# Content rows of attention made two groups at a time and moved on the chip by DMA

## What is computed

```python
h = layernorm(x) * (1 + ca) + sa
x = x + ga * attention(h)          # 16 heads, 16 content and 64 rope columns each, causal
h = layernorm(x) * (1 + cb) + sb
x = x + gb * ffn(h)                # 8 chosen experts of 96, weighted by a router
```

## Time and profile before

| | us |
|---|---|
| median of 3 runs | 1072.28 (1072.27 to 1074.97) |
| the profiled execution | 1072.48 |
| its span, first to last instruction | 1070.4 |
| PE busy | 1007.9 (94%) |
| DVE busy | 767.8 (72%) |
| ACT busy | 403.3 (38%) |
| POOL busy | 413.9 (39%) |
| mean granted TensorE clock | 0.981 |

### The profile page before, as it was taken

One profiled execution on the slowest core, in us unless ns is written; L12 is line 12 of the kernel. 1 busy time (PEld: TensorE's weight loads), 2 busy tenths in 40 slices (PEclk: granted clock), 3 DMA queues, 4 the chain that ended last, 5 costly groups with the idle time before them and its releaser, 6 DMA issues.

```text
span 1070.4 us, 24879 instructions
## 1 busy us (share of the span) xinstructions
PE 1007.9 (94%) x9783; PEld 735.9 (69%) x9783; DVE 767.8 (72%) x1518; ACT 403.3 (38%) x731; POOL 413.9 (39%) x357
## 2 busy tenths in 40 slices
PE   5979989999899999999899998999999998999888
PEld 4656667766686667766677666876768766776566
DVE  6767688586967868677776769768686777866454
ACT  4334533254314443145341643235431444315320
POOL 1526442264405454055432634145540644316200
PEclk9989999999999998999899999999999999999999
DMA  6220000200002000200002000020001000010000
GB/s 195 60 90 2 2 1 1 70 2 2 1 2 70 2 1 1 70 2 2 1 1 71 1 2 1 1 71 1 2 1 43 29 2 1 1 50 2 2 1 20
DMA packets 22232, 23.59 MB, mean 22 GB/s; under 512 B 6314, under 2 KB 20138, under 8 KB 22130
## 3 DMA queue, kind: packets, MB, share of 16 engines
q1 hardware_dynamic: 22130, 22.02, 6.7%
HBM read 17.80 MB, written 4.21 MB: 21 GB/s over the span
## 4 chain that ended last, share of the span: by engine, by line
PE 72%; DVE 11%; issue 8%; POOL 4%; ACT 3%; DMA 1%; POOLq 0%; DVEq 0%; SPq 0%; ACTq 0%
PE ring L1158 15%; PE ring L1006 11%; PE ring L1007 9%; PE ring L1008 9%; PE ring L1235 8%; PE av L1174 7%; PE ring L1130 5%; DVE mcol L888 2%; ACT pt L694 2%; POOL prod L564 2%; DVE xr L927 2%; PE ring L1142 2%; PE av L1187 1%; PE ring L1224 1%; DVE room L908 1%
## 5 line engine op out<-in xcount | busy, mean ns | idle before, releaser
L694 ACT ACTIVATE pt<-ring 128x384 f32<-128x384 f32 (+1 forms) x384 | 170.8, 532 | 316.9 <-PE ring L1158 281.2
L579 POOL TENSOR_SCALAR_AFFINE_SELECT pt<-pt 128x512 f32<-128x512 f32 x128 | 79.5, 637 | 391.9 <-ACT pt L694 391.9
L864 DVE TENSOR_TENSOR prod<-ring,table 128x1024 f32<-128x1024 f32 x128 | 155.5, 1218 | 92.7 <-PE ring L1008 92.1
L888 DVE TENSOR_REDUCE mcol<-ring 128x1 f32<-128x128 f32 (+3 forms) x512 | 211.4, 481 | 12.8 <-PE ring L1135 9.6
L1158 PE MATMUL ring<-rows 32*128 32x512 f32 (+3 forms) x3072 | 177.3, 331 | 10.0 <-ACT pt L694 5.0
L1158 PEld LDWEIGHTS ring<-rows 32*128 32x128 f32 x3072 | 131.6, 184 | 61.6 <-issue 30.0
L570 POOL TENSOR_TENSOR rows<-prod,rows 128x1024 fp32r<-128x1024 f32 x64 | 152.7, 2395 | 34.6 <-ACT rows L674 34.6
L563 POOL TENSOR_TENSOR prod<-prod 128x512 f32<-128x512 f32 x64 | 82.4, 1287 | 134.9 <-DVE prod L864 133.8
L1130 PE MATMUL ring<-rows 32*128 32x256 f32 (+3 forms) x1024 | 78.4, 356 | 21.6 <-ACT cont L686 6.9
L674 ACT ACTIVATE rows<-prod 128x1024 fp32r<-128x1024 f32 x64 | 67.6, 1063 | 58.3 <-PE ring L1158 36.9
L1130 PEld LDWEIGHTS ring<-rows 32*128 32x128 f32 x1024 | 44.5, 185 | 61.9 <-issue 42.2
(11 more groups left out here) (169 smaller groups left out, 1630.6 us busy)
## 6 DMA issues: line engine op xcount, KB each, us to landing
xn<-x_dram SPq DMA_DIRECT2D x8, 512.0 KB, 3.9
xr<-x_dram SPq DMA_DIRECT2D x8, 512.0 KB, 4.2
out_dram<-xr SPq DMA_DIRECT2D x8, 512.0 KB, 3.2
gate_bc<-gates_scratch SPq DMA_DIRECT2D x8, 256.0 KB, 4.8
pt<-wmod_dram SPq DMA_DIRECT2D x1, 1536.0 KB, 6.4
pt<-gup_t_dram SPq DMA_DIRECT2D x16, 96.0 KB, 2.5
dn<-wu_t_dram SPq DMA_DIRECT2D x1, 640.0 KB, 10.0
xr<-wk_t_dram SPq DMA_DIRECT2D x1, 512.0 KB, 8.2
```

The costliest lines, as they stand in the source:

```text
L694: sc.activation(pt[:, PT_AT[n] + h * w:PT_AT[n] + (h + 1) * w], ps[:, 0:w], ACT.Exp, scale=SCALE).then_inc(exp_ready.sem, 1)
L864: ve.tensor_tensor(prod[:, s % PROD, :, :], ps[:, :].unsqueeze(1).broadcast_to([P, 2, S]), table[:, :, :], ALU.mult).then_inc(rotated.sem, 1)
L888: last = ve.reduce_max(mcol[:, q, h * HR + HD:h * HR + HD + 1], ps[:, at:at + (q + 1) * P], AX_X)
```

## The change

1. The content columns are no longer laid out twice: `CON` is 256, and one `qcon` or `kcon` product (128 columns) holds two groups, the even group on even partitions and the odd group on odd ones. There are two of each for a block (p = 0, 1) instead of four.
2. `kcon_hi`/`kcon_lo` and `qcon_hi`/`qcon_lo` write hi and lo to `k_split` and `q_split`, which are the buffers `h2_hi` and `h2_lo` in the time in which the FFN does not use them. New steps `move_k` and `move_q` on SP, one of each for every group, copy every second partition to `cont`, three DMAs of 64 rows of 2 KB (128 KB) each.
3. `wofold` (POOL) multiplies `wo` by the gate into `wo_gated` (in the buffer `xn`), once for a block; `mixed` only adds.
4. The three orders are new, and blocks 1 to 6 are generated one after the other instead of a hardware loop. `load_late` gathers the late loads of the setup behind the first moves.

The diff, cut to its core:

```diff
-CON = NG * P
+CON = H * HD
+NBLK = CON // P
 SETUP_ORDER
-... kcon.00 kcon_hi.00 kcon_lo.00 ... qcon.00 qcon_hi.00 qcon_lo.00 ... kcon.01 kcon_hi.01 kcon_lo.01 hi.010 maxima.000 ... fuse.4 fuse.5 qcon.01 qcon_hi.01
-qcon_lo.01 shift.00 shifted.00 hi.011 lo.011 spread. split_ffn.0 split_ffn.1
+... kcon.00 kcon_hi.00 kcon_lo.00 move_k.00 ... qcon.00 qcon_hi.00 qcon_lo.00 move_q.00 rope.0101 rotate.0101 combine.010 values.00 values_out.00 values.01 values_out.01 move_k.01 hi.010 maxima.000 ... fuse.4 fuse.5 move_q.01 shift.00 shifted.00 hi.011 lo.011 spread. split_ffn.0 split_ffn.1 load_late.
 BODY_ORDER
-load_next.1 loads.0 maxima.010 rope.0200 reduce.010 score.000 ... combine.021 value.000 value.001 reduce.012 score.002 hi.020 shift.01 qcon.02 lo.020 exp.002 kcon.02 ...
+rope.0200 score.000 rotate.0200 load_next.1 rope.0201 exp.000 score.001 rotate.0201 clear.000 stats1.1 value.000
+exp.001 maxima.010 kcon.01 pow1.1 reduce.010 rope.0210 kcon_hi.01 clear.001 combine.020 score.002 rotate.0210
+kcon_lo.01 value.001 exp.002 maxima.011 hi.020 rope.0211 reduce.011 clear.002 maxima.012 rotate.0211 qcon.01
+reduce.012 combine.021 rope.0300 qcon_hi.01 shift.01 lo.020 value.002 shifted.01 qcon_lo.01 score.010 move_q.02
+attn_out.00 rotate.0300 rope.0301 loads.0 move_k.02 exp.010 score.011 rotate.0301 hi.021 clear.010 exp.011 maxima.020
...
+value.021 reduce.031 maxima.032 rope.1000 wofold.0 reduce.032 score.022 rotate.1000 shift.03 exp.022 rope.1001
...
+qcon_hi.10 value.032 qcon_lo.10 kcon.10 move_q.10 attn_out.03 values.10 rope.1011 values_out.10 hi.100 mix.00
+rotate.1011 kcon_hi.10 lo.100 kcon_lo.10 mix.01 move_k.10 mixed.00 combine.101 move_q.11 rope.1100 mixed.01 move_k.11
+hi.101 stats2.0 rotate.1100 pow2.0 maxima.100 lo.101 norm2.0 rope.1101 reduce.100 turn2.00 turn2.01 values.11
...
+wo_gated = xn[:, 0:NPAIR, :]
+k_split, q_split = h2_hi, h2_lo
+        def split_free(e, moved, b, ahead, p):
+            if p:
+                wait(e, up_used, b, ahead - 1, FT - 1)
+            for par in range(2):
+                wait(e, moved[par], b, ahead if p else ahead - 1, 2 if p else 3 * NBLK - 1)
-                with e.Fori(1, B - 1) as b:
+                for b in range(1, B - 1):
 SP
+                    elif kind in ("move_k", "move_q"):
+                        g = step[2]
+                        par, p = g % 2, g // 2
+                        if part != "setup":
+                            heads_free(sp, b, part, ahead, g)
+                            sp.sem_inc(waits_passed, 1)
+                        src, lo_made, moved = (k_split, k_lo, k_moved) if kind == "move_k" else (q_split, q_lo, q_moved)
+                        wait_alone(sp, lo_made, b, ahead, p)
+                        hi, lo = (src[par:P:2, i, :].bitcast(F32) for i in range(2))
+                        to = ((0, 0, hi), (1, 0, lo), (0, 1, hi)) if kind == "move_k" else ((0, 2, hi), (1, 2, hi), (0, 3, lo))
+                        for row, part_of, rows_of in to:
+                            sp.dma_start(cont[row:P:2, par, part_of, :].bitcast(F32), rows_of).then_inc(moved[par].sem, 16)
 POOL
+                    elif kind == "wofold":
+                        if part == "last":
+                            wait_alone(pool, lo_ready[1], b, ahead - 1, EC - 1)
+                        else:
+                            wait_alone(pool, lo_ready[0], b, ahead + 1, EC - 1)
+                        pool.tensor_tensor(wo_gated, wo[:, :, :], gate_bc[:, 0:E].unsqueeze(1).broadcast_to([P, NPAIR, E]),
+                                           ALU.mult).then_inc(wo_ready.sem, 1)
 ACT, modulate2
+                            else:
+                                wait(sc, k_moved[0], b, ahead + 1, 2)
+                                wait(sc, k_moved[1], b, ahead + 1, 2)
 ACT, kcon_hi
-                        sc.activation(cont[:, g % 2, 1, :], ps[:, :], ACT.Identity, scale=keep16, bias=one16)
-                        sc.activation(cont[:, g % 2, 0, :], ps[:, :], ACT.Copy, scale=sgn16).then_inc(k_scaled.sem, 1)
+                        split_free(sc, k_moved, b, ahead, p)
+                        sc.activation(k_split[:, 0, :], ps[:, :], ACT.Copy).then_inc(k_hi.sem, 1)
 ACT, exp
+                        if isinstance(b, int) and b == 0 and g == 0 and n == 0:
+                            sc.wait_ge(ffn_split, EC)
 DVE, start
+            for part_of in (1, 3):
+                ve.memset(cont[:, :, part_of, :].bitcast(F32), 0.0)
 DVE, kcon_lo
-                        ve.scalar_tensor_tensor(cont[:, g % 2, 0, :], ps[:, :], rest16, cont[:, g % 2, 0, :].bitcast(F32),
-                                                ALU.mult, ALU.add).then_inc(k_ready.sem, 1)
+                        ve.tensor_tensor(k_split[:, 1, :], ps[:, :], k_split[:, 0, :].bitcast(F32), ALU.subtract)\
+                          .then_inc(k_lo.sem, 1)
 DVE, mixed
-                        ve.tensor_tensor(sum2[:, :, :], ps[:, :].rearrange("p (t e) -> p t e", t=2), gate, ALU.mult)\
-                          .then_inc(mix_gated.sem, 1)
-                        ve.tensor_tensor(xr[:, 2 * i:2 * i + 2, :], xr[:, 2 * i:2 * i + 2, :], sum2[:, :, :], ALU.add)\
-                          .then_inc(mix_added.sem, 1)
+                        ve.tensor_tensor(xr[:, 2 * i:2 * i + 2, :], xr[:, 2 * i:2 * i + 2, :],
+                                         ps[:, :].rearrange("p (t e) -> p t e", t=2), ALU.add).then_inc(mix_added.sem, 1)
 PE, maxima
-                            wait_latest(pe, b, [(q_hi, ahead, g), (rope_hi, ahead, 2 * g + 1), (k_ready, ahead, g)])
+                            wait_latest(pe, b, [(q_moved[g % 2], ahead, 3 * (g // 2) + 2), (rope_hi, ahead, 2 * g + 1),
+                                                (k_moved[g % 2], ahead, 3 * (g // 2) + 2)])
```

More of the change, by code:

```diff
@@ L78 @@
 SETUP_ORDER = """
[L79 to L83, removed]
@@ L85 @@
 """
 BODY_ORDER = """
[L87 to L106, removed]
@@ new lines @@
+reduce.012 combine.021 rope.0300 qcon_hi.01 shift.01 lo.020 value.002 shifted.01 qcon_lo.01 score.010 move_q.02
+attn_out.00 rotate.0300 rope.0301 loads.0 move_k.02 exp.010 score.011 rotate.0301 hi.021 clear.010 exp.011 maxima.020
+value.010 reduce.020 clear.011 combine.030 maxima.021 rope.0310 reduce.021 lo.021 score.012 norm1.1 rotate.0310
+rope.0311 exp.012 move_k.03 maxima.022 move_q.03 rotate.0311 clear.012 turn1.10 reduce.022 combine.031 turn1.11
+value.011 modulate1.10 hi.030 shift.02 value.012 shifted.02 hi.031 low1.10 score.020 modulate1.11 attn_out.01
@@ L109 @@
+upped.01 ex.0 hi.111 top2.0 shift.10 lo.111 tanh.02 gate.03 gated.02 gate.04 tanh.03 upped.02 gated.03 turn_w.0
+tanh.04 gate.05 upped.03 wT.0 gated.04 wT_lo.0 up.04 tanh.05 shifted.10 weigh.00 up.05 weighed.00 gated.05 weigh.01
+upped.04 weigh.02 weigh.03 weighed.01 weigh.04 weigh.05 down.00 weighed.02 upped.05 weighed.03 weighed.04 weighed.05
+down.01 join.00 join.01 store.0
 """
 LAST_ORDER = """
- loads.0 maxima.010 rope.0200 reduce.010 score.000 rotate.0200 rope.0201 exp.000 rotate.0201 maxima.011 rope.0210
@@ L113 @@
[L113 to L122, removed]
@@ L128 @@
-store.0
+kcon.01 qcon.01 score.000 qcon_hi.01 kcon_hi.01 kcon_lo.01 qcon_lo.01 rope.0200 exp.000 maxima.010 rotate.0200
+clear.000 rope.0201 reduce.010 score.001 rotate.0201 rope.0210 exp.001 maxima.011 rotate.0210 clear.001 value.000
+combine.020 reduce.011 maxima.012 value.001 reduce.012 score.002 shift.01 exp.002 move_k.02 rope.0211 shifted.01
+hi.020 loads.0 move_q.02 clear.002 score.010 rotate.0211 combine.021 value.002 rope.0300 exp.010 attn_out.00 lo.020
+score.011 hi.021 rope.0301 exp.011 rotate.0300 clear.010 maxima.020 rotate.0301 clear.011 lo.021 value.010 reduce.020
@@ new lines @@
+maxima.021 rope.0310 combine.030 reduce.021 rope.0311 rotate.0310 wofold.0 score.012 rotate.0311 combine.031
+maxima.022 exp.012 move_q.03 hi.030 move_k.03 value.011 reduce.022 clear.012 hi.031 lo.030 value.012 shift.02
+maxima.030 shifted.02 score.020 reduce.030 attn_out.01 score.021 exp.020 maxima.031 clear.020 exp.021 maxima.032
+reduce.031 clear.021 lo.031 value.020 reduce.032 score.022 shift.03 exp.022 value.021 shifted.03 score.030 clear.022
+value.022 score.031 exp.030 attn_out.02 clear.030 exp.031 value.030 score.032 clear.031 warm.01 exp.032 value.031
@@ L424, in take_banks @@
             wait_latest(e, b, [u for u in used if u is not None and u not in SETUP_READ] + list(also))
-            return [bank(part, PLACES[part][0][step]) for step in steps]
+            return [bank(b, part, PLACES[part][0][step]) for step in steps]
         def take_bank(e, b, part, step, also=()):
@@ L847, in program @@
                         wait(ve, turned[i], b, ahead, c)
+                        if i == 1 and c == 0:
+                            for par in range(2):
+                                if part == "last":
+                                    wait(ve, q_moved[par], b, ahead, 3 * NBLK - 1)
+                                else:
```

(1 more changed line is left out.)

198 lines of the change are left out of this document (100 added, 98 removed).

## The result

The changed kernel took 1088.20 us (median of 4 runs, 1087.42 to 1088.79), the kernel before beside it 1073.62. The ratio is 1.0147 (95% interval 1.0126 to 1.0168): 15 us slower, where 25 us faster was forecast. The work did shrink.

A forecast was written before the change was run, and what follows sets the result against it. PE's work was taken to bound each block. From 1072.48 us, products -29.8, gate products -1.4, moves +5.6 and setup +0.8 gave 1047.7 for the profiled execution, 1047.5 us as median; range 1030 to 1066.

The forecast's parts named there:

- The moves: Copies into cont: each takes 3.4 us from release to landing, and PE waits for them at its group's maxima.
- +5.6: At maxima.020: PE waits 0.8 us for the moves in each of seven blocks, +5.6 us in all.
- Net 0: At maxima.100: PE's wait stays about the 1.00 us it has for ACT, net 0.
- -1.4: Block 7, chain mix, mixed, norm2: two gate products come off the path, -1.4 us.
- Products, -29.8: In all blocks: 128 fewer qcon and kcon matmuls at 0.233 us each take 29.8 us off PE.
- upper bound of 14: At maxima.020: if move_k.02 queues behind the 768 KB of loads.0, a wait of 2.0 us, +14 in all.
- the bound of 1: At maxima.100: the wait may change by -1 to +1 us a block around net 0.
- Setup, +0.8: At maxima.000: about +2.3 us for the move of q, less a 1.48 us content-product wait, net +0.8.
- the gain that the prediction named for `score.000`: Setup: score.000 no longer stands behind maxima.010, perhaps some 4 us; queueing behind expert loads may cost as much.
- Loop and other evictions, 0: Blocks: dropping the loop counts nothing, 2 us at most; fewer ACT and DVE evictions inside blocks count nothing.
- rival A: Moves come late, at two places in seven blocks and the setup: copies not overlapping or slow, 1082 to 1116 us; chance 0.11.
- Rival B: Between mix and turn2: removed products were filler, half the 16 matmuls become waiting, 1062 us; chance 0.13.

The follow-up runs named there:

- experiment 6: Changed kernel with move_k for group 2 issued earlier and POOL's lo.101 placed behind and made to wait for norm2: 1046.90 us, 0.9763 of the kernel before.
- experiment 8: Changed kernel with move_k for group 2 issued earlier and the query's first setup content product ahead of hi.001: 1054.41 us, 0.9843 of the kernel before.
- experiment 4: Kernel before, with blocks 1 to 6 generated one after the other instead of the hardware loop: 1071.90 us, 1.0003 of the kernel before.
- experiment 7: Changed kernel with move_k for group 2 issued earlier and rope.1101 put ahead of maxima.100: 1089.09 us, 1.0145 of the kernel before.

## Why the prediction was wrong

The step that failed is **"The moves"** and its "+5.6" for `maxima.020`, which measured about 27; "Net 0" for the stretch from `maxima.100` to `turn2` failed by 14, and the last block, with the tail's "-1.4", by some 5.

- **Products, -29.8: right.** Line 1120 has 16 matmuls instead of 32, PE's busy time fell by 26 us in spite of a lower clock, and with both new waits out of the way (experiment 6) block 4, at a clock of 1.00 in both, took 121.8 us instead of 125.1.
- **Moves at `maxima.020`, +5.6: about 27.** The place was right, PE's arrival too (5.4 against 5.7 us). The price of the queue was not: I took 0.47 us an issue from plain loads, the moves' issues took 0.60 (median), and in block 2 the first three took 2.77 us, where the others take 1.75 (in blocks 4 and 6 2.65 and 2.68). So the last of the eight was issued 5.3 us after the first, not 3.3. `move_k` then landed 3.0 to 3.5 us after its issues, behind the loads. That made the wait 25.3 us in all, 3 to 4 in blocks 0 to 6, past my upper bound of 14. And I gave a wait no price beyond its length: the slow matmuls behind it cost 1.7 us more in block 2. The move of k needed nothing of what stood ahead of it in SP's list; I listed the issues without asking that.
- **`maxima.100` and `turn2`, 0: about 14.** At `maxima.100` the wait is 1.41 us where it was 1.00, on `hi.101`, not on the moves. That is 0.4 us a block, within the bound of 1. The cost came where I had seen none: with the new order `lo.101` and the norm met. Before, `turn2` started without a wait, and I expected the chain ahead of it to get shorter, since it lost its gate products. It did lose them, and lost 2 us to POOL.
- **Setup, +0.8: one step wrong, the sum not settled.** The move of q was issued at 45.29, not 43.5: `qcon_hi.00` stood behind `hi.001` on ScalarE, and I had left its way to `qcon_lo.00` out of the walk; an earlier issue is worth some 5 us (experiment 8). On the other side the first exponential came 4.4 us earlier than before (68.51 against 72.87), the size of the gain that the prediction named for `score.000` and left out of its sum. With both new waits gone the store of block 0 is at 192.6, 1 us ahead of the forecast.
- **Tail, -1.4, and the products of block 7: not seen.** Block 7 became longer (118.8) or stayed (116.2), where 111.7 was forecast. The gate products are gone, but `turn2` starts 11.4 us after `mix` instead of 10.0. The start of `mix` before, and after:

```profile
1019.84 1.99 PE L1187 MATMUL av<-wo,room 128*128 128x256 f32 x8 [0.75 <-DVE room L912]
```

```profile
1033.62 3.75 PE L1218 MATMUL av<-xn,room 128*128 128x256 f32 x8 [2.42 <-DVE room L948]
```

PE waited 2.42 us instead of 0.75, and the eight matmuls took 3.75 us, where 1.97 is usual in a block. The new `LAST_ORDER` has `warm.01` ahead of the last values; before, its six matmuls (1.65 us) stood between these and `mix` and filled that stretch. That this ate the gate products and part of the gain in products is likely, but no run puts `warm.01` back.

- **Loop and other evictions, 0: right** (experiment 4).

With the two waits removed, 27 + 14 us, the kernel takes 1046.9 us against the 1047.5 of the forecast. That they agree is luck: the forecast holds 5.6 us for the first of these waits, and without them it is 1041.9. So of the 40.7 us between forecast and result some 21 are the wait at `maxima.020`, 14 the norm, and 5 remain, about what the last block has too much (116.2 against 111.7 in the profiled execution of experiment 6).

By its own signs the prediction was wrong where stores lie over 125 us apart (127.1 on the mean of blocks 1 to 6); the sign of the setup, a first exponential later than 76 us, did not come. The idle PE of more than 2 us at `maxima.020` is the sign that it gave for rival A. Rival A had the place and the side right, and the wrong mechanism: the copies overlapped and landed in 2.0 us (median), shorter than my 2.5; the queue of issues and the loads ahead of them were what was long. Rival B's place (`mix` to `turn2`) was right too, with a collision instead of missing filler.

## What to carry to other kernels

When a step becomes a DMA, write down what stands ahead of it in the issuing engine's list and issue it as soon as its own inputs are there; here one token moved up was worth 27 us. Price a wait of PE by its length and by the slow matmuls behind it, and do not push two short waits together (experiment 7 lost 27 us). When an order is rewritten, check which GpSimd and VectorE operations come to lie side by side, and whether the steps that kept PE busy still stand where it waits.
